# Row maxima as the bias of sixteen exponentials: one fused transformer kernel, softmax stage

## The reference, cut to what matters

```python
qr, kr = apply_rope(q, cos, sin), apply_rope(k, cos, sin)
scores = jnp.einsum('bhqd,bhkd->bhqk', qr, kr) / np.sqrt(HD) + mask   # mask: causal
attn = jax.nn.softmax(scores, axis=-1)
out = jnp.einsum('bhqk,bhkd->bhqd', attn, v)
out = out.transpose(0, 2, 1, 3).reshape(B, Sq, Dm)
return out @ Wo.T
```

## Time and profile before

| | |
|---|---|
| median of 3 runs | 903.14 us (902.97 to 904.03) |
| span of the profiled execution, first to last instruction | 900.1 us |
| what lies around the span (median less span; the profiled execution has no time of its own beside its span) | 3.0 us |
| mean granted TensorE clock | 0.999 of full |
| attention stage, steps 2 to 31 | about 435 to 657 us of the span |

### The profile page before, as it was taken

The page is one execution under the profiler, slowest core; times in us unless marked ns, Lnnn a source line. Parts: engine busy times, 40 slices in busy tenths (PEclk is TensorE's granted clock), DMA queues, the critical chain, the costliest instruction groups (busy, mean ns, idle before and its releaser), DMA issues.

```text
span 900.1 us, 24902 instructions
## 1 busy us (share of the span) xinstructions
PE 876.6 (97%) x10982; PEld 764.2 (85%) x10982; DVE 435.7 (48%) x931; ACT 203.0 (23%) x369; POOL 399.1 (44%) x310
## 2 busy tenths in 40 slices
PE   3899999999999999999999999999999999999998
PEld 3898999988888888888777777777789999999998
DVE  7455551111222222259887777788524433334444
ACT  4455542100000000023222332233331101011110
POOL 3343664203555556569978888877511000000000
PEclk9999999999999999999999999999999999999999
DMA  3789877211224222156544454544452121222201
GB/s 99 176 207 203 212 179 196 73 58 59 71 72 112 73 71 71 47 182 177 141 141 135 153 156 158 160 150 125 142 190 74 48 95 71 72 72 71 94 25 71
DMA packets 89723, 105.36 MB, mean 117 GB/s; under 512 B 42896, under 2 KB 57616, under 8 KB 89616
## 3 DMA queue, kind: packets, MB, share of 16 engines
q1 hardware_dynamic: 86624, 102.73, 39.2%
q10 hardware_dynamic: 2480, 0.51, 0.3%
q0 software_dynamic: 512, 0.53, 0.2%
HBM read 74.08 MB, written 29.65 MB: 115 GB/s over the span
## 4 chain that ended last, share of the span: by engine, by line
PE 91%; SPq 4%; DMA 3%; DVE 1%; issue 1%; ACT 0%; DVEq 0%
PE ps L939 24%; PE ps L1402 21%; PE ps L1211 20%; PE ps L632 7%; PE ps L903 5%; PE ps L1167 3%; PE ps L1147 3%; SPq L589 3%; PE ps L643 3%; PE ps L1375 2%; DMA toep<-kpad 2%; PE ps L1425 1%; PE ps L1426 1%; SPq L576 1%; DMA kpad<-ksb 1%
## 5 line engine op out<-in xcount | busy, mean ns | idle before, releaser
L1402 PE MATMUL ps<-wb,xf 128*128 128x420 f32 (+1 forms) x1152 | 195.7, 330 | 0.0
L1402 PEld LDWEIGHTS ps<-wb,xf 128*128 128x128 f32 x1152 | 188.3, 188 | 2.9 <-issue 0.2
L939 PE MATMUL ps<-y_hi,w_hi 128*128 128x512 f32 x320 | 125.0, 391 | 0.0
L939 PE MATMUL ps<-y_lo,w_hi 128*128 128x512 f32 x320 | 124.5, 389 | 0.0
L939 PE MATMUL ps<-y_hi,w_lo 128*128 128x512 f32 x320 | 124.5, 389 | 0.0
L1211 PE MATMUL ps<-y_hi 128*128 128x512 f32 x256 | 103.1, 403 | 0.0
L632 PE MATMUL ps<-xc,toep 64*128 64x192 f32 (+4 forms) x1088 | 96.8, 330 | 3.8 <-DMA toep<-kpad 3.8
L1211 PE MATMUL ps<-y_hi,y_lo 128*128 128x512 f32 x256 | 100.0, 390 | 0.0
L1211 PE MATMUL ps<-y_lo,y_hi 128*128 128x512 f32 x256 | 99.9, 390 | 0.0
L632 PEld LDWEIGHTS ps<-xc,toep 64*128 64x128 f32 x1088 | 90.9, 187 | 7.2 <-issue 4.9
L1047 POOL TENSOR_TENSOR rot<-rot,cst 128x512 f32<-128x512 f32 x40 | 52.7, 1319 | 72.9 <-DVE rot L1017 72.9
(11 more groups left out here) (153 smaller groups left out, 1260.2 us busy)
## 6 DMA issues: line engine op xcount, KB each, us to landing
toep<-kpad SPq DMA_DIRECT2D x124, 136.0 KB, 4.0
xc<-in_dram SPq DMA_DIRECT2D x32, 256.0 KB, 4.7
q_rows<-rf SPq DMA_DIRECT2D x32, 256.0 KB, 2.6
q<-q_rows SPq DMA_DIRECT2D x16, 512.0 KB
xr<-in_dram SPq DMA_DIRECT2D x16, 512.0 KB, 4.1
x_scratch<-xr SPq DMA_DIRECT2D x16, 512.0 KB, 2.9
x<-x_scratch SPq DMA_DIRECT2D x16, 512.0 KB, 3.6
out_dram<-x SPq DMA_DIRECT2D x15, 512.0 KB, 2.6
```

The costliest lines, as they stand in the source:

```text
L939: mm = pe.matmul(kq_bank(n), w[a][:, j, :], yt[b][:, j, g * 512:(g + 1) * 512], start=(j == 0 and a + b == 0), stop=(j == NJ - 1 and a == 1))
L1402: mm = pe.matmul(joint_bank(i, piece)[:, 0:hi - lo], xf[i % 2][:, a, t, :], wb[t][:, w4_place(t, c), lo:hi], start=(t == 0 and a + c == 0) ...
```

## The change

Scores are written negated (scale by -1/sqrt(32), the mask subtracted), so the row maximum of the scores becomes the row minimum of what stands in the tile, again negated. `exponentials` computes exp(-1 x tile + bias) with that minimum as the bias. A call takes one bias value for each partition, so a unit takes 16 calls of 64 columns where it took one of 1024. `subtract_max` is gone from GpSimd. The semaphore `g_sub` is gone with it, and everything that waited for it waits for something else: `exponentials` for `v_max`, and SP's two waits ahead of `load_kv` and `load_q` for `a_exp`, with the same counts.

```diff
@@ qkv_rope_sin (GpSimd, tail of the QKV stage)
-                    subtract_max(gp, 0)
-                if lead == 1:
-                    subtract_max(gp, 1)
...
-                    subtract_max(gp, 2)
...
-                    subtract_max(gp, 3)
...
-                    subtract_max(gp, 4)
@@ attention_transfers (SP)
                 if ahead:
-                    sp.wait_ge(g_sub, 2 * i + 4)
+                    sp.wait_ge(a_exp, 2 * i + 4)
                     load_kv(sp, i + 3)
...
                 if ahead:
-                    sp.wait_ge(g_sub, 2 * i + 5)
+                    sp.wait_ge(a_exp, 2 * i + 5)
                     load_q(sp, i + 3)
@@ scale, maximum (VectorE)
-            v.scalar_tensor_tensor(sc[:, u % CR, :].rearrange("p (g k) -> p g k", g=4), ps[:, 0:4, 0:256], INV_SQRT,
-                                   across(causal[:].rearrange("p r k -> p (r k)"), 4), ALU.mult, ALU.add).then_inc(v_sc, 1)
+            v.scalar_tensor_tensor(sc[:, u % CR, :].rearrange("p (g k) -> p g k", g=4), ps[:, 0:4, 0:256], -INV_SQRT,
+                                   across(causal[:].rearrange("p r k -> p (r k)"), 4), ALU.mult, ALU.subtract).then_inc(v_sc, 1)
-            v.tensor_reduce(stat[:, u % CR, 0, :], sc_groups(u), AX_X, ALU.max).then_inc(v_max, 1)
+            v.tensor_reduce(stat[:, u % CR, 0, :], sc_groups(u), AX_X, ALU.min).then_inc(v_max, 1)
-        def subtract_max(gp, u):
-            gp.wait_ge(v_max, u + 1)
-            gp.tensor_tensor(sc_groups(u), sc_groups(u), along(stat[:, u % CR, 0, :], S), ALU.subtract).then_inc(g_sub, 1)
@@ exponentials (ScalarE)
-            act.wait_ge(g_sub, u + 1)
-            act.activation(sc[:, u % CR, :], sc[:, u % CR, :], ACT.Exp).then_inc(a_exp, 1)
+            act.wait_ge(v_max, u + 1)
+            for k in range(16):
+                ins = act.activation(sc_groups(u)[:, k, :], sc_groups(u)[:, k, :], ACT.Exp,
+                                     bias=stat[:, u % CR, 0, k:k + 1], scale=-1.0)
+            ins.then_inc(a_exp, 1)
@@ attention_scale (GpSimd)
-                if w > FIRST and u < NUNIT:
-                    subtract_max(gp, u)
```

More of the change, by code:

```diff
@@ L288, in build @@
             "a_w3", "v_w3", "g_w3")]
-        pe_s, v_sc, v_max, g_sub, a_exp, v_sum, v_rec, g_prob = [signal(n) for n in (
-            "pe_s", "v_sc", "v_max", "g_sub", "a_exp", "v_sum", "v_rec", "g_prob")]
+        pe_s, v_sc, v_max, a_exp, v_sum, v_rec, g_prob = [signal(n) for n in (
+            "pe_s", "v_sc", "v_max", "a_exp", "v_sum", "v_rec", "g_prob")]
         v_pt, pe_o, a_othi, v_otlo, pe_y, a_pr, g_x1 = [signal(n) for n in (
```

## The result

The changed kernel takes 972.04 us (median of 4, 971.43 to 976.84) against 903.59 for the kernel before (4 runs), so it is 68 us slower. The ratio is 1.078, 95% interval 1.075 to 1.081 (the two medians alone divide to 1.076). The forecast was 948, with 930 to 975 as range: the direction and the place hold, the size was 24 us short, and 972 lies outside the 940 to 962 that the forecast had as its own range. The profiled execution took 972.05 us with a span of 970.2.

The account below looks back on a forecast made before the run. The prediction took TensorE, busy 97% of the span, as the bound. Span 900.1 + 36.3 (waits on q) + 8.4 (clock) = 944.8, with 3.0 us around the span 948 us; range 930 to 975, to hold 8 in 10.

Parts of the forecast that it names:

- What bounds the kernel, and what the taken and added work costs: TensorE, busy 97% of the span, bounds; 61 us off GpSimd and work added to ScalarE count nothing by themselves.
- The price of a call: Exponentials on ScalarE: 16 overlapping calls, 0.242 us between starts, take 3.96 us a unit, 2.90 more than before.
- The loop scale, exponentials, sums, scale: Attention step, ScalarE and VectorE: with the longer exponentials this loop takes 7.3 of 7.38 us and just fits.
- The moved wait of SP: SP's load_q goes out 7.0 us later, lands 3.3 us after issue; TensorE waits 2.8 us in 12 pairs, 36.3 in all.
- `load_kv`'s own wait: SP's keys and values load: its wait moves from 503.02 to about 510.1, still hidden before scores at about 520.9.
- The clock: TensorE's clock halves after some of the 12 gaps: half of them, 1.4 us each, adding 8.4 us.
- Full clock: Rival: the gaps in attention are too short to lower TensorE's clock; 939 us, chance 0.28.
- Low clock after nearly every gap: Rival: TensorE at half clock for about half a projection, 2.7 us, after each gap; about 972 us, chance 0.12.
- Calls without overlap: Rival: exponentials take 5.3 us a unit, adding 32 us; about 972 at full clock, 980 with clock term, chance 0.06.
- a hidden load: Rival: q lands within 0.6 us of issue, so only the loop counts; 903 to 906 us, chance 0.04.
- faster: Rival: a call starts every 0.06 us, q lands in time; at best 902 us, chance 0.02.
- The forecast's own range: Range of the main case, a stall of 2.8 us a pair and some lost clock: 940 to 962, chance 0.45.

Follow-up runs that it names:

- experiment 1: Changed kernel with SP's waits ahead of both load_kv and load_q on the row maximum (v_max), the 16 calls kept: 908.32 us, ratio 1.0073.
- experiment 6: Changed kernel with both SP waits on v_max, and VectorE's gather indices and FFN weight splits moved between maximum and sums: 903.92 us, ratio 1.0028.
- Experiment 3: Changed kernel with the x1 store issued ahead of the wait for load_q instead of right behind that load: 970.71 us, ratio 1.0769.
- experiment 9: Changed kernel with only the wait ahead of load_kv moved to v_max, load_q still waiting for the exponentials: 972.50 us, ratio 1.0804.
- experiment 8: Changed kernel with only the wait ahead of load_q moved to v_max, load_kv still waiting for the exponentials: 929.54 us, ratio 1.0322.
- experiment 4: Changed kernel with 15 unread matmuls of 512 columns between values and scores in the 12 steps that wait for q: 956.93 us, ratio 1.0613.
- experiment 2: Kernel before with only SP's two waits moved from the subtraction to the exponentials, one call of 1024 columns kept: 921.20 us, ratio 1.0229.
- experiments 2 to 5: The fifth: changed kernel with the x1 store ahead of the wait for load_q and 10 unread matmuls in the gap: 952.51 us, ratio 1.0579.

## Why the prediction was right, and where its sizes were off

- *What bounds the kernel, and what the taken and added work costs.* Right. 61 us less on GpSimd and 90 us more on ScalarE come to 6.6 us once the waits are released early (experiment 1, 1.0073) and to some 2.5 with VectorE's extra work moved (experiment 6, 1.0028): not quite the nothing that I wrote, but not what the 68 us are.
- *The price of a call.* Right: 16 calls in 3.92 us, 0.239 us from start to start, against 3.96. The Trainium skill, "ScalarE: Activation LUTs", What ACT_TABLE_LOAD costs, gives 280 ns + 0.833 ns for each element for a call with a bias operand and 93 ns of overlap, which makes 240 ns; the trace agrees. The budget in its Rules for kernel authors, which I weighed at 5.65 us, is 1.7 us too high for such a run of calls.
- *The loop scale, exponentials, sums, scale.* Right at 7.3 of 7.38: in the changed kernel, `scale` at 506.15, `sums` at 511.96 and the reciprocal's end at 513.46 make 7.31. I left out what this means once the wait on q is gone (VectorE's extra work, about 4 us), since in the change TensorE is late there anyway. Experiments 1 and 6 show it.
- *The moved wait of SP.* Right in mechanism, place, number (12) and release time. Its size is the step that failed: "the transfer is seen in the traffic: [...] 3.3 us after the issue". It measured 4.4 to 4.7 in most pairs, for two reasons. In the changed kernel the x1 store is issued 0.43 us after the load, where it used to come 3.1 us after it. I had named this store as queued behind the load, but priced it at nothing. Experiment 3 shows it: without the store behind it the landing is 3.6 to 3.9. The other 0.5 us is a reading: I took the end of the bytes as the landing, and in experiment 3 the bytes also end 3.2 us after the issue, while `scores` starts at 3.7. That term, 30.9 + 5.4 = 36.3 us in the forecast, is 45.0 + 6.1 + 0.8 = 52 us.
- *`load_kv`'s own wait "still hidden".* Right for the change, where q's release is later anyway (experiment 9), but not by itself: experiment 8 gives it some 21 us over experiment 1. I had checked when keys and values are needed, not what stands behind them in SP's queue.
- *The clock.* The direction was right, the size 8.4 against 15 us by experiment 4 (17.8 us lie outside the waits over eleven pairs). I counted half of the gaps at 1.4 us, a share that I chose and no row gave. The gaps turned out 4 us instead of 2.8, and the clock was at half after all 12, for 3.4 us at nine and 6.8 at three. Nor is the 2.2 us from idle to fall of the earlier trace rows a fixed delay: in the change TensorE's last matmul before the gap ended at 500.78 and the clock fell at 505.4, 4.6 us later; in experiment 3 it was 1.9 us.
- *The rivals.* Full clock (939) is excluded by the windows. "Low clock after nearly every gap" had 972, and the clock was indeed low after every gap. But its total is right by luck: a clock term of 32 us against some 15 to 18, and a wait of 36 against 52. Calls without overlap and a hidden load are excluded by the rows above. Nothing came out faster.
- *The range.* 972 lies in 930 to 975 only because I had stretched it to the centres of the two dearer rivals, whose prices were not met. The forecast's own range, 940 to 962, was missed.

What stays open: what decides when the clock falls (experiment 3 had less idle time and lost more), the spread of the landing times from 3.6 to 7.2 us over pairs and kernels, and some 2.5 us by which experiment 6 stands above before.

## What to carry to other kernels

A semaphore that paces loads often stands for "about now" and not for data. When the instruction that raised it goes, put the wait on what is ready at the same time as before (here the row maximum), not on the next thing in the chain, and check every load behind that wait in its queue: two lines cost 62 of 68 us here, and 20 us on the kernel before with its short call (experiment 2). Price a load that has become critical with its new neighbours, since its old landing time was measured without them, and count to the landing, not to the last byte. And where TensorE stops for some microseconds, add the slow microseconds after it to the bill.

## What the runs showed of the hardware that I had not expected

- A load of 512 KB on SP's queue landed after 3.6 to 3.9 us in ten of twelve pairs of experiment 3, with no store close behind it, and after 4.4 to 4.7 in ten of twelve pairs of the change, with a store of 512 KB issued 0.43 us *behind* it. In experiment 8 ten of twelve took 5.3 to 7.1 us (here to the landing that the profile records), with 0.9 to 1.2 MB issued in the 3 to 5 us ahead and a store 0.4 to 1.9 us behind.
- The last bytes of such a load had passed 0.5 us before the engine that waited for it started (experiment 3, 501.2 and 501.71).
- A shorter gap can cost more clock than a longer one: 4.0 us between matmuls gave 3.4 us at half speed, 3.0 us gave 6.8. What goes with the longer stretch is not the gap's length but where the fall came. In the change and experiments 2 to 5, 8 and 9 together, every fall of the clock in these steps that came 1.0 us or more before the gap's end gave 6.8 us at half speed, and every one from 0.2 us before its end to 1.6 us after it gave 3.4. Why is not shown. In a stage with such gaps, a gain of 0.7 us a pair in the wait was worth nothing in the total (1.0769 against 1.0777).
- Products that nobody reads made the changed kernel 15 us faster (956.93 against 972.04 us).
